# Weighing and rounding gathered rows in one ScalarE pass, with the weight applied again on VectorE (second stage of a two-layer graph network)

## The reference, cut to what matters

```python
h = x @ weight_l
msgs = edge_val[:, None] * h[edge_col]
agg = jax.ops.segment_sum(msgs, edge_row, num_segments=N)
out = agg + bias_l
out = out + x @ weight_r + bias_r
...
h = jax.nn.relu(_bn(einsum(x, W1) + b1, g1, be1, m1, v1))   # 8 experts
h = jax.nn.relu(_bn(einsum(h, W2) + b2, g2, be2, m2, v2))
y = einsum(h, Wo) + bo
return einsum(y, w)                                         # w: softmax gate
```

## Time and profile before

| | us |
|---|---|
| three timed runs: median (lowest to highest) | 3012.72 (3002.51 to 3017.39) |
| the profiled execution: time, and its span in the trace | 3008.19, 3006.3 |
| second stage in the trace | about 420 to 1840 |
| busy over the span: PE, DVE, ACT, POOL | 2719.2 (90%), 2165.6 (72%), 1514.5 (50%), 1939.8 (65%) |

### The profile page before, as it was taken

One profiled execution on the slowest core, in us unless ns is written; L12 is line 12 of the kernel. 1 busy time (PEld: TensorE's weight loads), 2 busy tenths in 40 slices (PEclk: granted clock), 3 DMA queues, 4 the chain that ended last, 5 costly groups with the idle time before them and its releaser, 6 DMA issues. The chain is left out here.

```text
span 3006.3 us, 53462 instructions
## 1 busy us (share of the span) xinstructions
PE 2719.2 (90%) x18949; PEld 2484.4 (83%) x18949; DVE 2165.6 (72%) x5008; ACT 1514.5 (50%) x3146; POOL 1939.8 (65%) x1692
## 2 busy tenths in 40 slices
PE   5799935899999999999999993689999999999999
PEld 5789825788888888888888873689999999999998
DVE  8898836577777877877787655767777777777762
ACT  4377636788888888888888651111111111111111
POOL 0355557777777777777777204777777777777750
PEclk9999956899999999999999996789999999999999
DMA  2133454333333233333323105888888888788860
GB/s 73 6 80 77 91 141 143 92 97 94 96 108 110 79 111 111 97 94 109 107 81 108 46 22 159 210 209 201 215 215 207 208 206 211 195 204 208 203 153 15
DMA packets 241570, 390.22 MB, mean 130 GB/s; under 512 B 43258, under 2 KB 114834, under 8 KB 241042
## 3 DMA queue, kind: packets, MB, share of 16 engines
q0 software_dynamic: 163072, 310.24, 40.6%
q1 hardware_dynamic: 77940, 74.90, 7.9%
q10 hardware_dynamic: 288, 1.61, 0.1%
HBM read 343.43 MB, written 43.19 MB: 129 GB/s over the span
## 5 line engine op out<-in xcount | busy, mean ns | idle before, releaser
L1324 POOL DMA_INDIRECT f_got<-h_tab,list_cols x784 | 974.9, 1244 | 287.8 <-issue 220.2
L1994 POOL DMA_INDIRECT n_got<-h_tab,edge_cols x784 | 798.9, 1019 | 263.2 <-issue 232.3
L2046 ACT ACTIVATE n_hrh<-bank 128x512 fp32r<-128x512 f32 (+1 forms) x208 | 119.3, 574 | 924.5 <-PE bank L2116 924.5
L1609 DVE TENSOR_TENSOR f_hlo<-edge_cols,f_hhi 128x1024 fp32r<-128x1024 f32 (+1 forms) x208 | 241.8, 1162 | 300.0 <-ACT f_hhi L1414 299.4
L2095 PE MATMUL bank<-n_got,n_hot_h 128*128 128x256 f32 x1168 | 352.0, 301 | 70.1 <-DMA n_got<-h_tab,edge_cols 36.2
L1384 ACT ACTIVATE f_got<-f_got,list_cols 128x256 f32<-128x256 f32 x784 | 333.9, 497 | 150.2 <-DMA f_got<-h_tab,list_cols 150.1
L1495 PE MATMUL bank<-f_mhi,f_hot 128*128 128x256 f32 x1168 | 316.2, 304 | 80.8 <-DVE f_mlo L1603 80.8
L1409 ACT ACTIVATE edge_cols<-bank,f_shf,f_scl 128x512 f32<-128x512 f32 (+1 forms) x416 | 295.2, 744 | 118.5 <-PE bank L1315 84.8
L2096 PE MATMUL bank<-n_got,n_hot_h 128*128 128x256 f32 x1168 | 338.6, 290 | 0.0
L2097 PE MATMUL bank<-n_got,n_hot_l 128*128 128x256 f32 x1168 | 338.5, 290 | 0.0
L2197 DVE TENSOR_SCALAR n_hot_h<-list_cols,rel_f,edge_cols 128x256 fp32r<-128x256 f32 (+1 forms) x784 | 252.4, 389 | 117.2 <-PE bank L2097 117.1
(11 more groups left out here) (327 smaller groups left out, 7396.3 us busy)
## 6 DMA issues: line engine op xcount, KB each, us to landing
f_got<-h_tab,list_cols POOLq DMA_INDIRECT x784
n_got<-h_tab,edge_cols POOLq DMA_INDIRECT x784, 3.8
h_tab<-acc SPq DMA_DIRECT2D x37, 128.0 KB
edge_cols<-in_w SPq DMA_DIRECT2D x16, 256.0 KB, 3.2
xn<-acc_tab SPq DMA_DIRECT2D x8, 512.0 KB, 5.8
n_rows<-acc_tab SPq DMA_DIRECT2D x8, 512.0 KB, 5.6
out_rows<-n_rows SPq DMA_DIRECT2D x8, 512.0 KB, 4.6
acc<-in_x SPq DMA_DIRECT2D x4, 896.0 KB, 8.4
```

Source lines behind the costliest of these rows:

```text
L1324: nc.gpsimd.indirect_dma_start(got[:, s % RING0, u, :], None, h_tab[0], bass.IndirectOffsetOnAxis(gidx0[:, s * U + u:s * U + u + 1], 0), b ...
L1609: nc.vector.tensor_tensor(hlo[l][:, :, 0:w], rl[:, :, 0:w], hhi[l][:, :, 0:w].bitcast(F32), ALU.subtract).then_inc(s_lo[l], 1)
L1994: nc.gpsimd.indirect_dma_start(got[:, s % RING, u, :], None, h_tab[1], bass.IndirectOffsetOnAxis(gidx[:, s * U + u:s * U + u + 1], 0), bou ...
```

## The change

ScalarE's two passes over a group become one: each of the four rows is multiplied by its weight and written, rounded, into `mhi` directly; `got` keeps the unweighted row. The one activation of 128x1024 at line 1393 is gone, and so is the semaphore between the two passes. The four activations now also wait for PE to have finished with `mhi` of two groups before (`s_prod`), and they stand behind the first layer's `relus(0)` and in front of `xhi` and the gate's and the norms' activations. VectorE makes `mlo` with four instructions of 128x256, `got * weight - mhi`, in place of one of 128x1024.

```diff
--- before.py
+++ after.py
@@ -1128,7 +1128,6 @@
             def sb3(name, shape, dt=F32):
                 return c3.enter_context(nc.sbuf_tensor(f"f_{name}", shape, dt))
             s_got = [sem(f"f_got{r}") for r in range(RING0)]
-            s_msg = sem("f_msg")
             s_mhi = sem("f_mhi")
             s_mlo = sem("f_mlo")
             s_hot = sem("f_hot")
@@ -1376,21 +1375,16 @@
 
             @block.scalar
             def _(act):
-                def weigh(s):
+                def upper_messages(s):
 
                     act.wait_ge(s_got[s % RING0], (s // RING0 + 1) * (16 * U))
+                    if s >= 2:
+                        act.wait_ge(s_prod, s - 1)
                     for u in range(U):
                         c = s * U + u
-                        last = nc.scalar.activation(got[:, s % RING0, u, :], got[:, s % RING0, u, :], ACT.Copy,
+                        last = nc.scalar.activation(mhi[:, s % 2, u, :], got[:, s % RING0, u, :], ACT.Copy,
                                                     scale=w0_f[:, c:c + 1])
-                    last.then_inc(s_msg, 1)
-
-                def upper_messages(s):
-
-                    act.wait_ge(s_msg, s + 1)
-                    if s >= 2:
-                        act.wait_ge(s_prod, s - 1)
-                    nc.scalar.activation(mhi[:, s % 2, :, :], got[:, s % RING0, :, :], ACT.Copy).then_inc(s_mhi, 1)
+                    last.then_inc(s_mhi, 1)
 
                 def relus(l, n):
 
@@ -1436,17 +1430,16 @@
                                              ACT.Copy).then_inc(s_upper, 1)
 
                 for s in range(AHEAD):
-                    weigh(s)
                     upper_messages(s)
                 for s in range(SLOTS):
                     if s in AT[2]:
                         relus(1, AT[2][s])
                     if s - 1 in USE_AT:
                         read_bank(USE_AT[s - 1])
-                    if s + AHEAD < EGROUPS:
-                        weigh(s + AHEAD)
                     if s in AT[0]:
                         relus(0, AT[0][s])
+                    if s + AHEAD < EGROUPS:
+                        upper_messages(s + AHEAD)
                     if s + 1 in FFN:
                         g = FFN.index(s + 1)
                         w = width(g) * P
@@ -1468,8 +1461,6 @@
                         t, w = tile(g, 0), width(g)
                         act.wait_ge(s_var4, g + 1)
                         nc.scalar.activation(scale[:, t:t + w], var[:, t:t + w], ACT.Sqrt).then_inc(s_sd4, 1)
-                    if s + AHEAD < EGROUPS:
-                        upper_messages(s + AHEAD)
                     if s == 1:
                         act.wait_ge(s_bn, 1)
                         nc.scalar.activation(scl[:, :, :, :], bnt[:, :, :, :], ACT.Sqrt).then_inc(s_bnroot, 1)
@@ -1600,8 +1591,12 @@
 
                 def lower_messages(s):
                     dve.wait_ge(s_mhi, s + 1)
-                    nc.vector.tensor_tensor(mlo[:, s % 2, :, :], got[:, s % RING0, :, :],
-                                            mhi[:, s % 2, :, :].bitcast(F32), ALU.subtract).then_inc(s_mlo, 1)
+                    for u in range(U):
+                        c = s * U + u
+                        last = nc.vector.scalar_tensor_tensor(mlo[:, s % 2, u, :], got[:, s % RING0, u, :],
+                                                              w0_f[:, c:c + 1], mhi[:, s % 2, u, :].bitcast(F32),
+                                                              ALU.mult, ALU.subtract)
+                    last.then_inc(s_mlo, 1)
 
                 def lower_half(l, n):
                     w = width(n // EXPERTS0) * P
```

## The result

The changed kernel took **3042.32 us** (median of 5, 3036.69 to 3042.87) beside 3012.72 of the kernel before: ratio 1.0094, 95% interval [1.0076, 1.0112]. It is slower, and the interval is clear of 1; I had forecast 2995 with 2974 to 3018. The profiled execution took 3042.87, its span is 3041.0.

The account below looks back on a forecast made before the run. TensorE was taken as the bound from 579 to 1683 us, GpSimd alone from 419 to 574. 3008.2 less 11 (stalls) less 4 (gathers) gave 2993 against the profiled execution; forecast 2995 us, range 2974 to 3018.

Parts of the forecast that it names:

- ScalarE's four activations at their old price: ScalarE, each slot: the four weighing activations stay at 1.71 us for four, with no price for rounded output.
- VectorE, 1.66 us for 1.22: VectorE's `mlo`: four instructions of 128x256 take 1.66 us in place of 1.22, +0.44 us in every slot.
- What the weight costs by slot: TensorE's stalls before E, per 16-slot group: slot 5 0.32, 7 1.28, 11 0.1, 15 1.0, 1 0.4 us.
- 1.5 as the limit: Slot 7, stall before E: the prediction is wrong if it loses more than 1.5 us.
- Slot 1's 0.4: Slot 1, stall before E: 0.4 us a group, as VectorE works without a gap and E had just arrived in time.
- L1's stalls gone: Second layer, even stretch: TensorE's waits for `hlo` vanish, booked as 9 us.
- 11: `xlo` comes early enough: Slot 11, before E: logit matmuls stand in between, so 0.1 us a group instead of about 1.2.
- The order of ScalarE as a gain: ScalarE, even slots: relus ahead of the weighing win up to 2.5 us in slot 4, 0.2 to 0.7 elsewhere, on `hlo`.
- The clock: TensorE, even stretch: granted clock read as 1.00, its upper level; no half-clock loss was booked.
- Early gathers: GpSimd, 419 to 574 us: gathers get in between the four `mlo` instructions, -4 us; otherwise +8.
- the sign of being wrong at 1.4: GpSimd: the prediction is wrong if gathers starting under `mlo` take over 1.4 us.
- The slower rival: VectorE too late: slots 7, 11, 15 and 1 each lose 0.88 us, slot 5 0.32; 3039 us, chance 0.1.

Follow-up runs that it names:

- u: Changed kernel with `mlo` unweighted in one subtraction, written over `got`, four `got` and three `mhi` entries, weighing ahead of `relus(0)`; ratio to the kernel before 0.9940.
- r_again: Repeat of the changed kernel with `mlo` written over `got`, four `got` and three `mhi` entries, weighing ahead of `relus(0)`; ratio to the kernel before 1.0009.

## Why the prediction was wrong

Step by step:

- *ScalarE's four activations at their old price*: right, 1.69 to 1.71 us for four with rounded output.
- *VectorE, 1.66 us for 1.22*: right, 477 ns each, 1.66 us from the start of the first to the end of the fourth.
- *What the weight costs by slot*: mostly right. Slot 5 0.34 each (booked 0.32), slot 7 1.43 (booked 1.28, and I had named 1.5 as the limit), slot 15 0.99 (1.0). Slot 1's 0.4 did not appear. Measured alone (`u` to `r_again`, on two chips) the weight costs 0.7%, 21 us, of which some 15 are stalls in slots 7 and 15.
- *L1's stalls gone*: right, no wait for `hlo` is left.
- ***"11: `xlo` comes early enough": the step that failed.*** I booked 0.1 for slot 11 and measured 2.33 us a group; 2.2 x 10.5 = 23 us. I said that `xhi` loses a pass in front or behind. Slot 8's pass stood in front of it, but slot 8's weighing (1.71 us) moved into its place, so that ScalarE came to slot 9's weighing 0.2 us later than before (in `r_again`, without the move, 1.0 us earlier). Slot 9's pass stood behind `xhi` and could give it nothing. And the weighing of slot 9 waits for a gather, which came 1.3 to 1.5 us later. I had listed what is queued behind the moved activations, and not asked what their own input would do. This names where the time is lost; it is not a cure, since on chip 15 after with `xhi` first had slot 11's stall before E gone and the time all but the same.
- *The order of ScalarE as a gain.* I priced the old order by the 2.24 us that ScalarE waited for the DMA and missed what it filled: the relus wait for `hlo` all the same, and the weighing used that time. Now that wait is 139.3 us and the weighing comes after it. The 9 us of L1 did come back; the order as a whole measured +0.7%, where I had booked them as its gain.
- ***The clock*: the second step that failed**, a term put at nothing without a reason. In the even stretch 12 to 27 us more were lost at 1.2 GHz than before (the two profiled executions of after differ in it by 15, and their spans, 3041.0 and 3026.8, by 14).
- *Early gathers*: -2 us instead of -4. From 419 to 574 us a gather takes 1169 ns instead of 1176; one that starts under the four short instructions does get in at their boundaries (1.22 us on average, where I had put the sign of being wrong at 1.4). But 31 of them began there up to 574 us, where I had counted on 21, and together they lost 6.7 us where before lost 8.3.

Slot 11 and the clock together are most of the miss. With slot 11 at 2.3 the sum would have been 3.2 - 0.1 + 2.3 = 5.4 us a group instead of 4.3: 12 us of loss, 8 with the 4 of the early gathers, and 20 to 35 with the clock; measured were 30. The slower rival had the right size (3039) and by half the wrong mechanism: slots 11 and 15 did stall 1.0 and 0.8 us more behind a VectorE without a gap, but slots 7 and 1 did not lose the 0.88 us that it asked of them, it had no term for the clock, and so its size was partly luck. The removed pass had no price of its own in my sum; where the old order stays it is worth up to 0.6% (18 us), the deeper rings included.

## What to carry to other kernels

An instruction that waits for a DMA ahead of others may be standing in time that is idle anyway: before moving it, look at what the others behind it wait for. When a pass is removed, see on which side of the late instruction it stood. Price a new stall of a TensorE that runs close to full with the half-clock stretch that can follow it, and treat a ratio from a single chip as that chip's where its trace shows waits that the traces of other chips do not have. Where gathers start under a long VectorE instruction with two SBUF inputs, try it in shorter pieces: here that won 0.4% on one chip, and lost 1.3% on a disturbed one.

## What the runs showed of the hardware

- Stalls of TensorE were in many cases followed by 3.4 us at 1.2 GHz, which lost 1.71 us each; from 579 to 1729 us that made 30.6 us in one execution of after, 15.3 in another, 3.4 in before.
- A gather took 1.01 us when it started with VectorE idle (236 in before, 419 to 1683 us) or under line 1626, which has one input in PSUM (110), and 1.71 on average when it started under `mlo`, whose two inputs are in SBUF (99).
- Splitting this 128x1024 subtraction in four made it 0.21 us longer (1.43) and the kernel 0.4% faster, and GpSimd's gathers got 7% shorter (1255 to 1173 ns).
- On two of the four chips of the experiments the same program ran 5.7 to 7.3% longer, with waits of up to 5.8 us on VectorE and ScalarE in before's trace that follow no releaser the profile shows. On one of them the same edit measured 1.0130 that measured 0.9960 elsewhere.
